# A sandwich of attention and a mixture of experts: weights split by VectorE in attention's last iteration, all L clips on GpSimd, three gathers per slot, and another order of the shared units

## The reference

```
x = x + layernorm(attention(layernorm(x)))       # 16 heads of 8, elu+1, rope, softmax, plus a 3-tap convolution of v
x = x + layernorm(ffn(layernorm(x)))
ffn:  scores = softmax(x @ gate_w.T); the 2 best of 8 experts by scores + gate_b, weighted by their scores
      h = (x @ w1.T + b1) * (x @ w3.T + b3)       # 256 columns: even ones g, odd ones l
      a = min(g, 7) * sigmoid(1.702 * min(g, 7)) * (clip(l, -7, 7) + 1)
      y = a @ w2.T + b2
      out = weighted sum of the two routed experts' y, plus the same from one shared expert
```

## Time and profile before

| | before |
|---|---|
| median of 3 runs | 1266.2 us (1265.22 to 1266.6) |
| profiled execution, its own time | 1265.12 us |
| its span, first to last instruction | 1263.3 us |
| mean granted TensorE clock | 0.943 of full speed |
| busy: PE, DVE, ACT, POOL | 1059.5, 1071.7, 937.9, 833.7 us |
| attention's stage ends, experts' begins | about 884 us |
| slot 0 of experts (start of its G product) | 889.69 us |
| stream 0's gathers | 1047.90 to 1160.99 us |
| stream 1's gathers | 1185.09 to 1248.93 us |

### The profile page before, as it was taken

How to read it: one execution, slowest core, us unless ns; L and a number is a source line. 1 busy time by engine, 2 the same in 40 slices (tenths; PEclk the granted TensorE clock), 3 DMA queues, 4 the chain that set the end, 5 groups by cost and what they waited for, 6 DMA issues and landing times. The chain is left out here.

```text
span 1263.3 us, 21973 instructions
## 1 busy us (share of the span) xinstructions
PE 1059.5 (84%) x6376; PEld 445.4 (35%) x6376; DVE 1071.7 (85%) x2451; ACT 937.9 (74%) x1782; POOL 833.7 (66%) x1087
## 2 busy tenths in 40 slices
PE   1498989999999999999998999898799999887810
PEld 0012222222322222222222222222578778655600
DVE  2398899999999999999999999991687889999944
ACT  1117888888888878788788788889699898867712
POOL 5445466676578787888778878645364546776475
PEclk9559999999999999999999999999799999999965
DMA  2453332422423334234233242203134544454412
GB/s 67 116 133 122 97 87 65 107 83 74 115 69 111 90 99 115 79 102 120 68 103 104 78 110 84 73 19 111 51 100 137 192 157 156 129 152 132 120 51 80
DMA packets 108982, 128.20 MB, mean 101 GB/s; under 512 B 14224, under 2 KB 81844, under 8 KB 108596
## 3 DMA queue, kind: packets, MB, share of 16 engines
q1 hardware_dynamic: 98848, 105.94, 29.5%
q0 software_dynamic: 8192, 16.79, 4.7%
q10 hardware_dynamic: 1824, 4.06, 0.9%
HBM read 58.85 MB, written 59.51 MB: 94 GB/s over the span
## 5 line engine op out<-in xcount | busy, mean ns | idle before, releaser
L1075 DVE TENSOR_REDUCE MX<-psS 128x1 f32<-128x512 f32 x1024 | 647.0, 679 | 64.8 <-PE psS L762 63.0
L974 ACT ACTIVATE PR<-psST 128x512 f32<-128x512 f32 x986 | 535.9, 600 | 127.3 <-PE psST L750 125.2
L762 PE MATMUL psS<-KS,QS 48*128 48x512 bf16 x1024 | 371.3, 400 | 40.8 <-DMA KS<-scratch_parts 23.8
L750 PE MATMUL psST<-QS,KS 51*128 51x512 bf16 x986 | 337.6, 385 | 42.3 <-ACT PR L974 25.8
L776 PE MATMUL psPV<-PR,V 128*32 128x512 f32 x2048 | 274.3, 608 | 5.8 <-ACT PR L974 1.0
L750 PEld LDWEIGHTS psST<-QS,KS 51*128 51x128 bf16 x986 | 78.5, 93 | 398.9 <-ACT PR L974 370.0
L1968 POOL DMA_INDIRECT SHARED<-scratch_y,FROM x128 | 130.2, 1017 | 51.6 <-issue 37.9
L465 POOL DMA_INDIRECT scratch_x<-XN,POSI x128 | 128.6, 1005 | 36.3 <-issue 34.0
L762 PEld LDWEIGHTS psS<-KS,QS 48*128 48x128 bf16 x1024 | 87.8, 93 | 105.5 <-DVE MX L1075 73.5
L1533 PE MATMUL psY<-WD,HA 128*128 (+1 forms) x496 | 67.7, 279 | 13.3 <-issue 6.9
L1507 PE MATMUL psH<-XH,WS 128*128 128x512 f32 x169 | 74.0, 438 | 2.9 <-DVE XL L1720 2.0
(11 more groups left out here) (217 smaller groups left out, 1845.7 us busy)
## 6 DMA issues: line engine op xcount, KB each, us to landing
scratch_parts<-PT SPq DMA_DIRECT2D x192, 128.0 KB, 2.4
QS<-scratch_parts SPq DMA_DIRECT2D x64, 192.0 KB, 3.3
KS<-scratch_parts SPq DMA_DIRECT2D x64, 192.0 KB, 4.2
XR<-scratch_x SPq DMA_DIRECT2D x46, 256.0 KB, 2.8
scratch_y<-YR SPq DMA_DIRECT2D x46, 256.0 KB, 2.0
RES<-EL SPq DMA_DIRECT2D x64, 128.0 KB, 2.0
scratch_x<-ZERO SPq DMA_DIRECT2D x18, 256.0 KB
X<-in_x SPq DMA_DIRECT2D x16, 256.0 KB, 4.7
```

The costliest lines, as they stand in the source:

```text
L750: nc.tensor.matmul(bank(st_banks(t), k)[:], KS[t.par][rows, h // 2, kc * P:(kc + 1) * P], QS[t.par][rows, h // 2, :], start=True, stop=Tru ...
L762: nc.tensor.matmul(bank(psS, k)[:], QS[b.par][rows, h // 2, qc * P:(qc + 1) * P], KS[b.par][rows, h // 2, :], start=True, stop=True).then_ ...
L974: nc.scalar.activation(PR[:, s % 2, HEAD_AT[j], :], bank(st_banks(t), k)[:], ACT.Exp, scale=SCALE).then_inc(st_exp, 1)
L1075: nc.vector.tensor_reduce(out=MX[:, qc, h:h + 1], in_=bank(psS, k)[:], axis=AX.X, op=ALU.max).then_inc(s_max, 1)
```

## The change

Four edits. (1) DVE does both parts of the split of all nine experts in attention's last iteration, one expert's high part and the previous one's low part per slot from slot 1, in `SPLIT_ORDER`; `WALL` is allocated first and lies over attention's `COS`, `SIN`, `XT`, `EXQ`, `EL`, `RES`, `QS0` and `KS0`, whose last readers `wall_free` waits for. (2) POOL clips L up to `LAST[1]`, the last routed unit of stream 1, not `LAST[0]`. (3) Stream 0's gathers go at three per slot; stream 1's still at four. (4) `FRONT`, `MIXED` = 2, 6, which leaves eight S at the end. With these, R26 lies in slot 28 and R45 in slot 53; gathers begin at slots 32 and 57; `FINISH` is 35, 38, 41, 43, 46, 49, 51, 54, 57, 59 and then 60, 62, 64, 66, 68, 70; roots stand in slots 40, 45, 51, 56, 61, 64, 68, 70, 72 (before: 40, 44, 48, 52, 56, 66, 70, 72, 74).

```diff
@@ attention
-        COS = sb("COS", [P, N], F32)
-        SIN = sb("SIN", [P, N], F32)
+        COS = beneath_wall(0, "COS", [P, N], F32)
+        SIN = beneath_wall(ROW_BYTES, "SIN", [P, N], F32)
...
+            SPLIT_ORDER = (NE, *range(NE))
+
+            def wall_free():
+                dve.wait_ge(st_psum, (B - 1) * TILES)
+                dve.wait_ge(vT_psum, B)
+                for w in range(2):
+                    dve.wait_ge(turned[w], 32 * B)
+                    dve.wait_ge(rot_cos[w], B)
...
+            def weights_high(n):
+                e = SPLIT_ORDER[n]
+                for m, W in enumerate((W1, W3)):
+                    last = nc.vector.tensor_copy(WALL[:, e, 0, m], W[:, e].rearrange("p (f g) -> p g f", g=2))
+                last.then_inc(high, 1)
+
+            def weights_low(n):
+                e = SPLIT_ORDER[n]
+                dve.wait_ge(high, n + 1)
+                for m, W in enumerate((W1, W3)):
+                    last = nc.vector.tensor_tensor(WALL[:, e, 1, m], W[:, e].rearrange("p (f g) -> p g f", g=2),
+                                                   WALL[:, e, 0, m].bitcast(F32), ALU.subtract)
+                last.then_inc(split, 1)
+
             def iteration(t):
                 nxt = t + 1
                 for s in range(SLOTS):
                     for j in range(HG):
+                        if t.c == B - 1 and j == 2 and 1 <= s <= EXP_ALL + 1:
+                            if s == 1:
+                                wall_free()
+                            if s <= EXP_ALL:
+                                weights_high(s - 1)
+                            if s > 1:
+                                weights_low(s - 2)
@@ experts
-        SPLIT_AT = (0, 4, 8)
-        FRONT, MIXED = 3, 7
-        PACE = 4
+        FRONT, MIXED = 2, 6
+        PACE = (3, 4)
...
         def pool_clips(p):
-            return p <= LAST[0]
+            return p <= LAST[1]
...
-                        pe.wait_ge(split, 1)
+                        pe.wait_ge(split, EXP_ALL)
...
-            weights_high(NE)
             turn(0)
...
-                if p + 1 < len(SPLIT_AT):
-                    for e in range(SPLIT_AT[p], SPLIT_AT[p + 1]):
-                        weights_high(e)
                 if routed(p + 2):
                     stage(ORDER[p + 2][1])
...
-            weights_low(0, NE)
             turn(0)
             ends.normalise(dve, Batch(B - 1), 1, psG)
...
-                if p + 1 < len(SPLIT_AT):
-                    for e in range(SPLIT_AT[p], SPLIT_AT[p + 1]):
-                        weights_low(e + 1, e)
                 drain(p)
...
-                    for n in range(PACE * (p - GATHER_AT[st]), PACE * (p - GATHER_AT[st] + 1)):
+                    for n in range(PACE[st] * (p - GATHER_AT[st]), PACE[st] * (p - GATHER_AT[st] + 1)):
```

More of the change, by code:

```diff
@@ L469, in attention @@
 def attention(nc, ends, x_in, wqkvT, chan, ones, rope_cos, rope_sin, ident, numbers, count, gate_wT, gate_b,
-              X, WD, IDF, TAB, ZERO, BD, XN2, CW, BASE, XG, scattered, zero_filled, weights, halved, table, load_weights):
+              X, WD, IDF, TAB, ZERO, BD, XN2, CW, BASE, XG, scattered, zero_filled, weights, halved, table, load_weights,
+              W1, W3, WALL, arena, split):
     nc.disable_value_cache = True
@@ L479, in sem, with beneath_wall @@
             return es.enter_context(nc.semaphore(name))
+        def beneath_wall(at, name, shape, dt):
+            return nc.alloc_sbuf_tensor_at(name, shape, dt, offset=arena + at)
         WQKV = sb("WQKV", [P, 3 * C], F32)
@@ L506, in attention @@
         MT = sb("MT", [PARTS * HALF, 2, N], BF16)
-        QS = [sb(f"QS{i}", [P, PAIRS, N], BF16) for i in range(2)]
-        KS = [sb(f"KS{i}", [P, PAIRS, N], BF16) for i in range(2)]
+        QS = [beneath_wall(10 * ROW_BYTES, "QS0", [P, PAIRS, N], BF16), sb("QS1", [P, PAIRS, N], BF16)]
+        KS = [beneath_wall(14 * ROW_BYTES, "KS0", [P, PAIRS, N], BF16), sb("KS1", [P, PAIRS, N], BF16)]
         V = [sb(f"V{i}", [P, QC, H, VW], F32) for i in range(2)]
@@ L522, in attention @@
         SCM = nc.dram_tensor("scratch_max", [2, 2, PARTS * HALF, N], BF16, kind="Internal").ap()
+        high = sem("weights_high")
         consts = sem("consts_loaded")
@@ L1244, in unit_tables, with experts @@
         nc.vector.tensor_scalar(ROW[:, units], UNIT[:, 0:UNITS[st]], float(ROOM * NE), None, ALU.min).then_inc(row_ready, 1)
-def experts(nc, ends, W1, W3, WD, BD, halved, X, IDF, TAB, ZERO, XN2, POS, WSEL, CW, CNT, XG, XTD, scattered,
+def experts(nc, ends, W1, W3, WALL, split, WD, BD, halved, X, IDF, TAB, ZERO, XN2, POS, WSEL, CW, CNT, XG, XTD, scattered,
             zero_filled, table, BASE, DROP, EXPERT, ROW, expert_ready, row_ready, out):
@@ L1285, in experts @@
         FIRST_B = [0, SPAN]
-        FINISH = [GATHER_AT[int(b >= SPAN)] + (GATHERS * (b - FIRST_B[int(b >= SPAN)] + 1)) // PACE + 1 for b in range(B)]
+        FINISH = [GATHER_AT[int(b >= SPAN)] + (GATHERS * (b - FIRST_B[int(b >= SPAN)] + 1)) // PACE[int(b >= SPAN)] + 1
+                  for b in range(B)]
         GROUPS = [(b, b + 1) for b in range(0, B - 2, 2)] + [(B - 2,), (B - 1,)]
@@ L1347, in experts @@
         count_ready, from_step = sem("count_ready"), sem("from_step")
-        high, split = sem("weights_high"), sem("weights_split")
         cw_psum, cwT_ready = sem("cw_psum"), sem("cwT_ready")
@@ L1580, in _ @@
         def _(act):
[L1581 to L1584, removed]
             def turned_gates(g, m):
@@ L1629, in evict @@
                     if i < R_EARLY:
-                        act.wait_ge(split, min(2 * (i // 2) + 3, EXP_ALL))
+                        act.wait_ge(split, EXP_ALL)
                     elif i < R_BUFS:
@@ L1704, in _ @@
         def _(dve):
[L1705 to L1710, removed]
             def turn(p):
@@ L2002, in sb @@
             return ctx.enter_context(nc.sbuf_tensor(name, shape, dt))
+        arena = -(-nc.sbuf_base // 32) * 32
+        WALL = sb("WALL", [P, EXP_ALL, 2, 2, 2, F], F32R)
+        split = ctx.enter_context(nc.semaphore("weights_split"))
         X = sb("X", [P, B * QC, C])
@@ L2050, in build @@
         attention(nc, ends, x, wqkvT, chan, ones, cos, sin, ident, table, count, gate_wT, gate_b,
-                  X, WD, IDF, TAB, ZERO, BD, XN2, CW, BASE, XG, scattered, zero_filled, weights, halved, unit_table, load_weights)
-        experts(nc, ends, W1, W3, WD, BD, halved, X, IDF, TAB, ZERO, XN2, POS, WSEL, CW, CNT, XG, XTD, scattered,
+                  X, WD, IDF, TAB, ZERO, BD, XN2, CW, BASE, XG, scattered, zero_filled, weights, halved, unit_table, load_weights,
+                  W1, W3, WALL, arena, split)
+        experts(nc, ends, W1, W3, WALL, split, WD, BD, halved, X, IDF, TAB, ZERO, XN2, POS, WSEL, CW, CNT, XG, XTD, scattered,
                 zero_filled, unit_table, BASE, DROP, EXPERT, ROW, expert_ready, row_ready, out)
```

16 lines of the change are left out of this document (10 added, 6 removed).

## The result

| | before | after |
|---|---|---|
| median | 1266.35 us (1265.22 to 1266.6, 4 runs) | 1276.51 us (1276.11 to 1277.86, 4 runs) |
| profiled execution, its span | 1265.12, 1263.3 us | 1276.11, 1274.3 us |
| granted TensorE clock | 0.943 | 0.966 |
| first gather; stream 1's first; end of gathers | 1047.90; 1185.09; 1248.85 us | 1052.53; 1188.91; 1259.83 us |

The changed kernel is **slower**: ratio 1.008, 95% interval 1.0068 to 1.0092. Forecast were 1261.6 us and a range up to 1267.5. The result lies outside, on the side of the first rival. (Stream 1's first gather is the 79th that POOL issues here and the 81st before, because two gathers of stream 0 are left for slot 58.

The account below looks back on a forecast made before the run. POOL's gather queue was taken to bound the end: 129.4 us from 1046.5 to stream 1's start at 1175.9, gathers ending 1244.3, then 14.4, span 1258.7, 4.6 less than 1263.3. Median forecast 1261.6 us, range 1255.5 to 1267.5.

Parts of the forecast that it names:

- first rival: "Handshake, slower": DVE's and POOL's waits for each other add up, w over 10; w = 12 gives span 1267.7; chance 0.14.
- split in attention: Attention's last iteration: DVE's copies and subtractions, 15 us at most, fit into its waits; cost 0, or 1.4 without cover.
- slots 0 and 1: Rounding and splitting leave these slots, so `XH` and `add_lepe` come earlier: 5.3 us saved, bounds 3 and 7.
- first gather: Slot 32: clip 32 now precedes it, so almost all of the 5.7 us lead is lost there; today 1047.90.
- 22 clips (the first ahead of the first gather): POOL's queue, slots 32 to 53: clips of 0.61 us and 0.09 around each, 15.4 us.
- 78 gathers: POOL's queue from slot 32 until stream 1's first gather: 1.32 us each, 103.0 us.
- four roots: POOL's queue from slot 32 until stream 1's first gather: four roots at 2.0 us each, 8.0 us.
- w: POOL's waits for a late L product from slot 32 until stream 1's first gather: between 0 and 8, taken as 3 us.
- first to 79th gather: POOL's stretch up to stream 1's first gather, forecast at 1175.9 us against 1185.09 before.
- 79th to end of gathers: Stream 1's 48 gathers and a root, 63.84 us, plus two leftover gathers and one root, 4.6; ends at 1244.3.
- behind it: From the end of gathers to the end of the span: the last 14.4 us stay.
- The dear clip: Rival, slower: DVE's work slows POOL's clips and roots by 1.54, 22 clips cost 7.3 us more; span 1266; chance 0.05.

Follow-up runs that it names:

- second session: Long-condition session; its run with four roots ahead of their slot's clip and gathers, against the changed kernel, took 1281.56 us, 0.9583 of before.
- fourth session: Short-condition session: changed kernel with gathers ahead of clip 1262.57 us, root ahead too 1267.43; the split alone 1261.8, and with gathers replaced by arithmetic 1243.07.
- the split alone: Kernel before plus only the split in attention's last iteration; clips, pace and order as before: 1348.37 us (0.994), 1330.25 (0.9942), 1261.8 (0.9975).
- a hold: POOL waits for the slot's product L before its gathers; without POOL's clip, on the changed kernel with DVE clipping, up to slot 53: 1300.57 us, 0.9583.
- A looser one: Changed kernel with DVE clipping, root ahead, POOL waiting before its gathers only for the previous slot's product L, up to slot 60: 1310.04 us, 0.9667.
- short condition: Sessions in which the kernel before runs fast, as in the result: its median was 1265.29 us in one of the five follow-up sessions.
- long condition: Sessions in which the kernel before runs slow: medians 1355.01, 1335.91, 1355.68 and 1355.77 us in four of the five follow-up sessions.

## Why the prediction was wrong

Its sum against the trace (the prediction's start of stream 1 is the 79th gather):

| term | forecast | after |
|---|---|---|
| split in attention | 0 | DVE's waits filled; slot 0 is 1.96 later, see below |
| slots 0 and 1 | 5.3 saved | 4.8 |
| first gather | 1047.2 | 1052.53 |
| 22 clips (the first ahead of the first gather) | 15.4 with gaps | 14.5 without |
| 78 gathers | 103.0 | 104.1 |
| four roots | 8.0 | 8.2 |
| w, the waits for L over 0.5 us | 3 | 9.5 in eight waits |
| first to 79th gather | 128.7 | 136.4 |
| 79th to end of gathers | 68.4 | 70.9 |
| behind it | 14.4 | 14.5 |

The miss of 15.6 us in the span is 5.3 at the first gather, 7.7 in the stretch, 2.5 in the rest, 0.1 behind. In the stretch, 6.5 of the 7.7 are w.

**The step that failed most is the paragraph on w.** It saw the right mechanism, gave it a range of 0 to 8, and put the break-even at 7.6; measured were 9.5. What it overlooked is the root. It counted roots as POOL's work alone, 2.0 us each. It didn't ask who waits for a root that stands behind three gathers: `shift`, and behind `shift` in DVE's queue the next L product, and for that the next clip. `shift` waited 4.89, 4.96, 1.23 and 1.85 us, and behind the first three of these the clip waited 1.59 us each: 4.8 of the 9.5. With the roots ahead (second session) two waits over 0.5 us are left of the eight, of 0.99 and 2.04 us. The other five waits, 4.7 us, are nearer to the forecast's 3. The trace of before had a hint. The prediction read from the earlier trace rows that DVE has no waits in these slots. A busy share doesn't say that: between 1040 and 1180 us DVE's `shift` waits for the root three times there, though briefly (us in total, times, longest):

```profile
DVE SH L1807 <- POOL RS L1982: 2.2, 3, 1.2
```

The paragraph also took POOL's backlog as cover ("DVE catches up with a POOL that is behind") without looking whether there is one: the queue begins with a clip for which POOL waits, so there is none. Three gathers ahead of that clip make the backlog, and the waits over 0.5 us among the gathers are gone. With that order the time is near the forecast, 1262.57 beside 1261.6, though the terms are not the same: the first gather is 1.4 us later than forecast, the stretch 1.2 longer and the rest 1.5.

**The second step that failed is the first gather**, 5.3 us of the miss. The paragraph on slots 0 and 1 let slots 2 to 27 only move, and the one on POOL's queue took the whole lead of 5.7 us off slot 32. That clip 32 stands ahead of it was foreseen. Its L product was forecast to end at 1046.5 and ended at 1051.2, 1.0 us before that of before. Of the 5.7 us of lead, 1.96 were gone at slot 0, 0.5 in the head, 0.6 in slots 2 and 3, 0.7 until slot 32; slot 32 is now a routed unit, whose L comes 2.28 us behind G instead of 1.78; and the 0.4 of DVE's lighter load didn't show. The clip itself then took 0.99 us. The 1.96 isn't the split's doing: DVE's steps ahead of its first copy are late by 1.8 already, and in the fourth session, with the same split, slot 0 begins at 889.94, 889.72, 890.14 and 891.34 (889.69 before).

**The rest**, 2.5 us: the 50 gathers from the 79th on come every 1.34 us and not every 1.29. Why they are slower wasn't looked into.

**Right were** the cost of the split in attention, the head (slot 2's G product lies 14.34 us behind slot 0's, forecast 13.8), the clip's price (0.66 us each for 0.61) and the gathers' pitch (1.34 for 1.32). The dear clip didn't come. The Trainium skill, page Perfetto Trace Analysis, section Optimizing Scalar/DVE Operations, warns of the read port that GpSimd and DVE share. The trace agrees for single instructions, as in the pair of copies that takes 1.47 us instead of 0.50 while POOL runs a two-input instruction (L1181), but it set no term of the sum. The rival **handshake, slower** (0.14) is what happened, with w at 9.5 instead of its 12, and with the root as a third wait beside the two that it named. Even its span, 1267.7, is 6.6 us short, for the first gather and the rest. It deserved more than 0.14: the prediction itself had no depth between the queues to set against it.

**What stays open.** Why the kernel before takes 70 to 90 us more in some sessions. Shown is, in the split alone, that most of this time lies in slots in which POOL issues gathers without a hold, and that up to slot 53 a hold removes the slow slots with or without clips. A looser one removes them in part. Up to 26 us of it lie in attention, ahead of all gathers, and nothing was tried on them. Whether any run of GpSimd instructions would do the same, and what the other engines lack in the meantime (their instructions, for one), isn't shown. Nor is it known what the third gather per slot and the new order are worth in the short condition without POOL's clips.

## What to carry to other kernels

When an engine gets a small task for another one into a queue of long instructions, write down the loop: who waits for the small result, what is queued behind that wait, and whether its end feeds the first engine again. If it does, give the first engine work that is ready between receiving and delivering: here the order "gathers, clip, root" instead of "clip, gathers, root" was worth 11 us between the profiled executions and 14 between the medians. Moving the small task ahead was worth 2.4 us in its stretch and nothing at the end, and on top of the new order it cost 4.9. And measure a close decision in more than one session: the same pair of kernels came out at 1.008 and at 0.959.

## What the runs showed of the hardware

- The same kernel on the same chip took 1265.29 us (median of 25) in one session and 1335.91 (of 13) in another; the changed kernel took 1276.51 and 1281.92 us, the one with the gathers ahead 1262.57 and 1294.29.
- In the long condition DVE stood for 15.06 and 9.40 us, ACT for 6.31 and PE for 6.24 within one slot, with no releaser that the profile shows, while POOL issued an indirect gather every 1.25 us (0.94 and a gap of 0.30). In the short condition the same kernel issues its first 32 gathers in a row without a wait, from 1044.36 to 1086.67, one every 1.36 us, and no slot is over 6.44 us.
- A split copy of 128x256 to fp32r takes 0.25 us on DVE (0.50 for the pair) and 0.74 beside POOL's two-input instruction (1.47 for the pair).
